# A four-layer hybrid model on one core: the experts' down product with split weights streamed per slot

## The chip, the cores and the metric

The program runs on one core of one Trainium2 chip. The metric is device time in microseconds, the median of the runs shown. The core has five engines with queues of their own: TensorE (PE; its weight loads are listed as PEld), VectorE (DVE), ScalarE (ACT), GpSimd (POOL) and SyncE (SP). They wait for each other through semaphores, and each runs its own instructions strictly in the order in which the program gives them.

## The reference, cut to what matters

The model has 4 x 1024 tokens of width 256 and four layers in a row, each with a residual sum: attention with low-rank adapters, an expert layer, a Mamba-2 layer, and the same expert layer again with the same weights. The expert layer is

```python
x = hidden_states.reshape(-1, d)               # 4096 x 256, normalised
logits = x @ Wr + br                           # 4 experts
probs = softmax(logits)
top_w, top_idx = top_k(probs, 1)               # one expert for each token
g = einsum('td,edf->tef', x, Wg)               # d = 256, f = 1024
u = einsum('td,edf->tef', x, Wu)
h = silu(g) * u
y = einsum('tef,efd->ted', h, Wd)
out = take_along_axis(y, top_idx) * top_w
```

The change concerns the product with `Wd` for the chosen expert, in both expert layers, and where its weights come from.

## The kernel before

`program` runs four phases one after the other: `attention`, `routed_ffn` (names with g1_), `mamba`, `routed_ffn` again (g2_). Each phase writes one instruction list per engine (`@block.sync`, `vector`, `gpsimd`, `scalar`, `tensor`), by hand; no planner is involved in the expert layers. In the profile's rows the names of both expert layers begin with g_.

**The expert layer** starts with a prologue: TensorE turns the tokens, the router's logits are formed, and VectorE works out to which of 35 slots (`SLOTS`) each token belongs. A slot is 128 tokens of one expert; 32 tiles of tokens and up to three partly filled ones give 35. Meanwhile SP loads the gate and up weights (8 MB) and, from L1024, the down weights of all four experts (4 MB) into `w_d`. ScalarE rounds the gate and up weights to the short form F32R (`w_hi`), and VectorE subtracts the rounded part, so that the rest (L1054) stands in F32R in `w_gu`: a full product is then formed from three short ones, high x high, high x low, low x high (`terms`, L1410 on).

Then the 35 slots follow. For slot j:
- POOL `fetch(j)` (L1240) gathers the slot's 128 token rows from DRAM, an indirect DMA with 128 indices.
- VectorE `stats(j)` (L1170 to L1172) forms mean and variance; POOL `root(j)` (through L90) forms the inverse root; VectorE `center(j)` (L1179) normalises.
- TensorE `turn(j)` (L1401) transposes the tokens; VectorE `take(j)` (L1184, L1186) splits them into high and low.
- TensorE `up(j)` (L1419) forms gate and up, 24 products of 512 columns; ScalarE `activate(j)` (L1319) and VectorE `combine(j)` (L1192) form the hidden values.
- TensorE `turn_hidden(j)` (L1441) transposes them in eight pieces into `ps_h`; VectorE copies one half (L1197), ScalarE the other (L1323) to `hid_t`.
- TensorE `down(j)` (L1433): eight products of 256 columns in full F32, each of which TensorE runs as two passes, so 16 instructions per slot. The expert's weights are picked in `w_d` through a register.
- VectorE `result(j)` (L1203) scales and adds the residual; POOL `send(j)` (L1247) scatters the rows to DRAM.

The order on each engine is a software pipeline. TensorE does up(j), down(j-1), turn(j+1), turn_hidden(j). VectorE does

```python
if j + 2 < SLOTS: stats(j + 2)
combine(j)                      # then take(j + 1), hidden(j), result(j - 1)
if j + 2 < SLOTS: center(j + 2)
```

and POOL does root(j+2), send(j-1), fetch(j+3). Four token buffers (`XE`), two result buffers and one buffer of hidden values set how far the engines can run ahead.

**The attention phase** has 16 units of 24 steps (`CORE`). In a step TensorE forms a pair of score products (L854), ScalarE takes two exponentials (L690), POOL masks on the diagonal (L576), and TensorE weighs the values (L870) four steps later; the probabilities stand in a ring of seven. VectorE meanwhile finds maxima of score chunks for later heads (L438, L442). In the last four units no query, key or value work for a later batch is left, so `raw`, `rope`, `x_t`, `xn` and `swapped` are unused after the fifth step of unit 12. POOL's `remainder` (L546) is a subtraction of 128 x 512 values; SP collects sums and results by DMA (`collect`, `gather_sums`, `store_inverse`, `spread_inverse`).

## Time and profile before

| | |
|---|---|
| median of 3 runs | 2194.78 us (2182.81 to 2199.73) |
| the profiled execution | 2185.0 us |
| its span, first to last instruction | 2183.1 us |
| busy: TensorE, VectorE, ScalarE, GpSimd | 1819.3, 1191.3, 822.7, 725.6 us |
| moved by DMA | 161 MB, mean 74 GB/s |
| mean granted TensorE clock | 0.901 of 2.4 GHz |

The busy times of different engines overlap. Idle time of an engine only costs something where the others wait for it. The attention phase ends at about 812 us, the first expert layer runs from 820 to 1245, the Mamba layer to about 1755, the second expert layer to the end.

### The profile page before, as it was taken

How to read it: one execution, taken by the hardware profiler on the slowest of the kernel's cores; microseconds unless marked ns; L12 is line 12 of the kernel's file. 1: busy time of each engine (PE TensorE's matmuls, PEld its weight loads, DVE VectorE, ACT ScalarE, POOL GpSimd, SP SyncE). 2: the span in 40 equal slices, each digit the busy share in tenths (PEclk: the TensorE clock that was granted, in tenths of full speed). 3: DMA queues.
4: the chain of work that ended last, by engine and by line, in shares of the span. 5: the costliest groups of instructions: out<-in, count | busy, mean ns of one | idle time of the engine just before them, and what ended most of it. 6: DMA issues, size and time to landing. Idle time of an engine off the chain costs nothing. (4 is left out here: it accounts for less than half of the span.)

```text
span 2183.1 us, 30159 instructions
## 1 busy us (share of the span) xinstructions
PE 1819.3 (83%) x9520; PEld 1212.1 (56%) x9520; DVE 1191.3 (55%) x2979; ACT 822.7 (38%) x1705; POOL 725.6 (33%) x922
## 2 busy tenths in 40 slices
PE   5368889889888864899999658989898938999997
PEld 3133334434433322788888535747484727888886
DVE  4466676666666508543443356665656685443442
ACT  2036655656665624111111035554646441111111
POOL 2335464464462312222222124333242312222221
PEclk9569989989988855999999969999999978999999
DMA  5522333332442108000000230100101080000000
GB/s 160 174 89 90 119 126 95 122 125 77 134 135 87 39 16 313 22 24 28 26 25 26 70 111 15 43 36 1 78 1 78 1 309 22 26 24 30 25 24 9
DMA packets 90179, 161.23 MB, mean 74 GB/s; under 512 B 23080, under 2 KB 50476, under 8 KB 88880
## 3 DMA queue, kind: packets, MB, share of 16 engines
q1 hardware_dynamic: 71504, 107.39, 14.7%
q0 software_dynamic: 17984, 50.62, 7.2%
q8 instruction: 86, 1.41, 0.3%
q10 hardware_dynamic: 544, 1.31, 0.2%
q14 instruction: 61, 0.50, 0.1%
HBM read 102.52 MB, written 45.48 MB: 68 GB/s over the span
## 5 line engine op out<-in xcount | busy, mean ns | idle before, releaser
L690 ACT ACTIVATE a_probs<-a_ps_e 128x512 f32<-128x512 f32 (+3 forms) x768 | 336.0, 491 | 204.1 <-PE a_ps_e L854 200.9
L438 DVE CUSTOM_DVE_ANT_0 a_ps_m<-a_ps_m,a_causal 128x512 f32<-128x512 f32 (+3 forms) x512 | 239.4, 517 | 97.5 <-PE a_ps_m L841 96.4
L1433 PE MATMUL g_ps_y<-g_w_d,x_res 128*128 x1120 | 253.2, 379 | 2.8 <-DVE x_res L1203 2.8
L854 PE MATMUL a_ps_e<-a_q_st,a_k_st 64*128 64x512 f32 (+3 forms) x768 | 187.9, 480 | 76.4 <-ACT a_probs L690 48.5
L854 PEld LDWEIGHTS a_ps_e<-a_q_st,a_k_st 64*128 64x128 f32 x768 | 79.6, 201 | 289.8 <-ACT a_probs L690 200.5
L1433 PEld LDWEIGHTS g_ps_y<-g_w_d,x_res 128*128 128x128 f32 x1120 | 212.3, 190 | 34.6 <-issue 3.2
L442 DVE TENSOR_REDUCE a_peak<-a_ps_m 128x1 f32<-128x512 f32 x256 | 164.8, 686 | 94.8 <-PE a_ps_m L841 94.1
L841 PE MATMUL a_ps_m<-a_k_st,a_q_st 64*128 64x512 f32 (+3 forms) x768 | 152.7, 399 | 68.8 <-DMA a_k_st<-a_scr_k 28.0
L1323 ACT COPY x_res<-g_ps_h 128x512 f32<-128x512 f32 x70 | 41.1, 587 | 439.2 <-PE g_ps_h L1441 439.2
L576 POOL TENSOR_SCALAR_AFFINE_SELECT a_probs<-a_probs 128x256 f32<-128x256 f32 x256 | 103.9, 408 | 284.1 <-ACT a_probs L690 283.8
L1170 DVE BATCH_NORM_STATS2 g_xe_stats<-x_res 128x6 f32<-128x256 f32 x70 | 29.9, 426 | 295.6 <-DMA x_res<-g_x_rows,g_token_i 295.6
L870 PE MATMUL a_ps_a<-a_probs,a_vals 128*32 128x512 f32 (+3 forms) x1536 | 185.7, 559 | 0.1
L1319 ACT ACTIVATE x_res<-g_ps_g 128x1024 f32<-128x1024 f32 x70 | 71.9, 1028 | 213.8 <-PE g_ps_g L1419 213.8
L841 PEld LDWEIGHTS a_ps_m<-a_k_st,a_q_st 64*128 64x128 f32 x768 | 84.4, 205 | 102.6 <-issue 44.5
L90 POOL TENSOR_TENSOR g_xe_rs<-g_xe_ve,table 128x1 f32<-128x1 f32 x70 | 39.2, 561 | 202.5 <-DVE g_xe_ve L1172 202.5
L1240 POOL DMA_INDIRECT x_res<-g_x_rows,g_token_i x70 | 77.6, 1108 | 84.0 <-DVE g_token_i L1145 63.5
L1192 DVE TENSOR_TENSOR x_res<-x_res,g_ps_u 128x1024 f32<-128x1024 f32 x70 | 85.5, 1221 | 27.3 <-PE g_ps_u L1419 27.3
L1419 PE MATMUL g_ps_g<-g_w_hi,g_xe_hi 128*128 x280 | 95.7, 423 | 1.7 <-DVE g_xe_hi L1184 1.7
L1773 POOL TENSOR_TENSOR m_y<-m_y,m_z_act 128x512 f32<-128x512 f32 x32 | 40.6, 1269 | 157.1 <-DVE m_y L1699 157.1
L1247 POOL DMA_INDIRECT g_y_rows<-x_res,g_token_i x35 | 36.6, 1044 | 168.2 <-DVE x_res L1203 163.4
L1247 POOL DMA_INDIRECT out<-x_res,g_token_i x35 | 36.6, 1044 | 168.1 <-DVE x_res L1203 168.1
L1624 DVE SCALAR_TENSOR_TENSOR m_conv<-m_pre,m_conv_w,m_conv 128x1024 f32<-128x1024 f32 x48 | 70.1, 1460 | 34.9 <-ACT m_conv L1827 34.0
(272 smaller groups left out, 3664.5 us busy)
## 6 DMA issues: line engine op xcount, KB each, us to landing
a_q_st<-a_scr_q POOLq DMA_DIRECT2D x32, 512.0 KB, 4.0
a_k_st<-a_scr_k POOLq DMA_DIRECT2D x32, 512.0 KB, 4.8
m_spread_acs<-m_acs_rows SPq DMA_DIRECT2D x8, 2048.0 KB, 9.7
a_scr_q<-a_high SPq DMA_DIRECT2D x36, 256.0 KB
a_scr_k<-a_high SPq DMA_DIRECT2D x36, 256.0 KB
a_swapped<-a_raw SPq DMA_DIRECT2D x64, 128.0 KB, 2.0
g_w_gu<-L_ffn_Wg SPq DMA_DIRECT2D x8, 1024.0 KB, 9.8
g_w_gu<-L_ffn_Wu SPq DMA_DIRECT2D x8, 1024.0 KB, 12.4
```

The source lines that it names most:

```text
L438: nc.vector.tensor_tensor_reduce(ps_m[:, bank, 0:w], ps_m[:, bank, 0:w], causal[:, 512 - w:], 1.0, MASKED, ALU.add, ALU.max, peak[:, p % 2 ...
L442: nc.vector.tensor_reduce(peak[:, p % 2, r, i, c:c + 1], ps_m[:, bank, 0:w], AX, ALU.max).then_inc(chunk_max, 1)
L576: nc.gpsimd.affine_select(tile, tile, [[0, 2], [1, P]], ALU.is_ge, 0.0, base=0, channel_multiplier=-1).then_inc(masked, 1)
L690: nc.scalar.activation(probs[:, N % RING, r, q0:], ps_e[:, (2 * N + r) % HEAD_BANKS, q0:], ACT.Exp, scale=DH ** -0.5).then_inc(exp_done, 1)
L841: nc.tensor.matmul(banks[r][:, 0:w], q_st[rows(r), p % BUFS, i * P:(i + 1) * P], k_st[rows(r), p % BUFS, 512 * c:512 * c + w], start=True, ...
L854: nc.tensor.matmul(ps_e[:, (2 * N + r) % HEAD_BANKS, q0:], k_st[rows(r), p % BUFS, j * P:(j + 1) * P], q_st[rows(r), p % BUFS, 512 * c + q ...
L870: last = nc.tensor.matmul(ps_a[32 * u:32 * u + 32, q0:], vals[:, b % 2, j, 17 * h:17 * h + 32], probs[:, (U * CORE + 2 * m + u // 2) % RIN ...
L1192: nc.vector.tensor_tensor(hid, gate, ps_u[:].rearrange("p b f -> p (b f)"), ALU.mult).then_inc(hid_ready, 1)
L1240: nc.gpsimd.indirect_dma_start(out=xe[:, j % XE], out_offset=None, in_=x_rows, in_offset=bass.IndirectOffsetOnAxis(ap=token_i[:, j:j + 1], ...
L1247: nc.gpsimd.indirect_dma_start(out=y_rows, out_offset=bass.IndirectOffsetOnAxis(ap=token_i[:, j:j + 1], axis=0), in_=rows[:, j % 2], in_of ...
L1419: last = nc.tensor.matmul(ps[:, c], x[:, d * P:(d + 1) * P], w[:, :, d].rearrange("p a f -> p (a f)"), start=(n == d == 0), stop=(n == len ...
L1433: last = nc.tensor.matmul(ps_y[:, 0:D], hid_t[:, f * P:(f + 1) * P], w_d[:, bass.ds(e, 1), f].rearrange("p a d -> p (a d)"), start=(f == 0 ...
```

## The change

The down product is formed from three short terms like the gate and up products. The split weights don't stay in SBUF: the attention phase prepares them once, in its last four units, in a DRAM table `down_rows` of 512 rows (one for each expert and partition) of 16 KB, in which a row holds, for each of eight tiles, 256 high and 256 low values. For each of four experts, SP loads 1 MB (`load_down`), ScalarE rounds four pieces of 128 x 512 (`round_down`), POOL subtracts four (`lower_down`), and SP stores 2 MB in three DMAs (`store_down`).

In the expert layers the load of `Wd` on SP goes. POOL gathers for each slot the 128 rows of its expert (2 MB, `stream`) by an indirect DMA into one of two buffers; the row numbers come from two new small steps on VectorE. `hidden` is now two copies on ScalarE, which round, and two subtractions on VectorE, each of which waits for its copy. `down` has eight products of 512 columns (high hidden x high and low weights side by side) and eight of 256 (low hidden x high weights); `result` adds both halves in two dependent steps. On VectorE the order becomes center(j+1), combine(j), take(j+1), hidden(j), result(j-1), stats(j+2); on POOL send(j-1), fetch(j+3), stream(j+1), root(j+2).

```diff
 # attention, SP, in the loop over units U and steps n
+                    if U * CORE + n in WD_AT:
+                        load_down(WD_AT[U * CORE + n])
+                    if U * CORE + n - 21 in WD_AT:
+                        store_down(WD_AT[U * CORE + n - 21])
+        WD_AT = {12 * CORE + 10 + 14 * e: e for e in range(EXPERTS)}
+            def load_down(e):
+                sp.wait_ge(low_ready, 4 * 2 * BATCH)
+                if e >= 2:
+                    sp.wait_ge(wd_out, 48 * (e - 1))
+                sp.dma_start(wd_raw[e % 2].rearrange("p (t d) -> p t d", d=D), A["Wd"][e].rearrange("(t p) d -> p t d", p=P)
+                             ).then_inc(wd_in, 16)
+            def store_down(e):
+                sp.wait_ge(wd_less, 4 * (e + 1))
+                sp.dma_start(wd_rows[e, :, :, 1], wd_raw[e % 2].rearrange("p (t d) -> p t d", d=D)).then_inc(wd_out, 16)
+                for k in range(2):
+                    sp.dma_start(wd_rows[e, :, 4 * k:4 * k + 4, 0], wd_high[e % 2][k].rearrange("p (t d) -> p t d", d=D)
+                                 ).then_inc(wd_out, 16)
+            def lower_down(e, k):                      # POOL, steps 11, 13, 15, 17 after the load
+                pool.wait_ge(wd_rounded, 4 * e + k + 1)
+                nc.gpsimd.tensor_tensor(part.bitcast(F32R), part, high_part, ALU.subtract).then_inc(wd_less, 1)
+            def round_down(e, k):                      # ScalarE, steps 8, 10, 12, 14 after the load
+                if k == 0:
+                    act.wait_ge(wd_in, 16 * (e + 1))
+                nc.scalar.copy(high_part.bitcast(F32R), wd_raw[e % 2][:, 512 * k:512 * k + 512]).then_inc(wd_rounded, 1)
...
 # expert layer, SP
-            sp.wait_ge(turned_ps, HALVES)
-            for e in range(EXPERTS):
-                sp.dma_start(w_d[:, e], F["Wd"][e].rearrange("(t p) d -> p t d", p=P)).then_inc(wd_in, 16)
 # VectorE
+            step(nc.vector.tensor_scalar(owner[:, 1, :], owner[:, 0, :], float(P), lanes[:, 0:1], ALU.mult, ALU.add))
+            nc.vector.tensor_copy(row_index[:], owner[:, 1, :]).then_inc(index_ready, 1)
             def hidden(j):
-                dve.wait_ge(ht_ps, j + 1)
-                nc.vector.tensor_copy(hid_t[:, 0:512], ps_h[:, 0]).then_inc(ht_lo, 1)
+                for c in range(2):
+                    dve.wait_ge(ht_hi, 2 * j + c + 1)
+                    some = slice(c * 512, (c + 1) * 512)
+                    nc.vector.tensor_tensor(hid_lo[:, some], ps_h[:, c], hid_hi[:, some].bitcast(F32), ALU.subtract
+                                            ).then_inc(ht_lo, 1)
             def result(j):
-                nc.vector.scalar_tensor_tensor(rows[:, j % 2], ps_y[:, 0:D], scale[:, j:j + 1], xe[:, j % XE], ALU.mult,
-                                               ALU.add).then_inc(row_sb, 1)
+                step(nc.vector.scalar_tensor_tensor(rows[:, j % 2], ps_y[:, 0:D], scale[:, j:j + 1], xe[:, j % XE],
+                                                    ALU.mult, ALU.add))
+                nc.vector.scalar_tensor_tensor(rows[:, j % 2], ps_y[:, D:2 * D], scale[:, j:j + 1], rows[:, j % 2],
+                                               ALU.mult, ALU.add).then_inc(row_sb, 1)
-            center(1)
             weights()
             for j in range(SLOTS):
-                if j + 2 < SLOTS:
-                    stats(j + 2)
+                if j + 1 < SLOTS:
+                    center(j + 1)
                 combine(j)
...
-                    center(j + 2)
+                    stats(j + 2)
 # POOL
+            def stream(j):
+                if j >= 2:
+                    pool.wait_ge(y_ps, j - 1)
+                nc.gpsimd.indirect_dma_start(
+                    out=w_d[:, j % 2].rearrange("p f d -> p (f d)"), out_offset=None, in_=C["wd_rows"],
+                    in_offset=bass.IndirectOffsetOnAxis(ap=row_index[:, j:j + 1], axis=0),
+                    bounds_check=EXPERTS * P - 1, oob_is_err=False).then_inc(streamed[j % 2], 16)
             root(0)
             root(1)
+            for j in range(2):
+                stream(j)
             for j in range(SLOTS):
-                if j + 2 < SLOTS:
-                    root(j + 2)
                 if j >= 1:
                     send(j - 1)
                 if j + 3 < SLOTS:
                     fetch(j + 3)
+                if 2 <= j + 1 < SLOTS:
+                    stream(j + 1)
+                if j + 2 < SLOTS:
+                    root(j + 2)
 # ScalarE
             def hidden(j):
                 act.wait_ge(ht_ps, j + 1)
-                nc.scalar.copy(hid_t[:, 512:1024], ps_h[:, 1]).then_inc(ht_hi, 1)
+                for c in range(2):
+                    nc.scalar.copy(hid_hi[:, c * 512:(c + 1) * 512], ps_h[:, c]).then_inc(ht_hi, 1)
 # TensorE, down(j)
+                w = w_d[:, j % 2]
+                pe.wait_ge(streamed[j % 2], sends(j % 2, j + 1))
                 for f in range(FT):
-                    last = nc.tensor.matmul(ps_y[:, 0:D], hid_t[:, f * P:(f + 1) * P],
-                                            w_d[:, bass.ds(e, 1), f].rearrange("p a d -> p (a d)"), start=(f == 0),
-                                            stop=(f == FT - 1))
+                    if f % 4 == 0:
+                        pe.wait_ge(ht_hi, 2 * j + f // 4 + 1)
+                    nc.tensor.matmul(ps_y[:], hid_hi[:, f * P:(f + 1) * P], w[:, f], start=(f == 0), stop=False,
+                                     skip_group_check=True)
+                for f in range(FT):
+                    if f % 4 == 0:
+                        pe.wait_ge(ht_lo, 2 * j + f // 4 + 1)
+                    last = nc.tensor.matmul(ps_y[:, 0:D], hid_lo[:, f * P:(f + 1) * P], w[:, f, 0:D], start=False,
+                                            stop=(f == FT - 1), skip_group_check=True)
```

## Rows read from the trace of the kernel before

**Rows 1.** Windows: stretch, its us, busy us of each engine, clock, DMA share, GB/s.
```profile
1000.00:1200.00 200.00, 199.37 (x984) 168.93 (x983) 81.11 (x176) 32.31 (x40) 52.13 (x59) 1.00 0.08 26
```

**Rows 2.** One slot in order of time: start, us, engine, line, operation [idle before].
```profile
1010.07 0.38 PE L1401 MATMUL g_ps_x<-table,x_res 128*128 128x128 f32 x2
...
1010.29 1.04 PE L1441 MATMUL g_ps_h<-table,x_res 128*128 128x128 f32 x8
...
1011.09 0.71 PE L1419 MATMUL g_ps_g<-g_w_hi,g_xe_hi 128*128 x2
1011.37 0.59 ACT L1323 COPY x_res<-g_ps_h 128x512 f32<-128x512 f32 x1 [6.31 <-PE g_ps_h L1441]
1011.37 0.69 DVE L1197 COPY x_res<-g_ps_h 128x512 f32<-128x512 f32 x1
...
1011.98 0.47 DVE L1203 SCALAR_TENSOR_TENSOR x_res<-g_ps_y,g_scale,x_res 128x256 f32<-128x256 f32 x1
...
1013.26 1.05 POOL L1247 DMA_INDIRECT g_y_rows<-x_res,g_token_i  x1 [4.47 <-DVE x_res L1203]
...
1014.61 1.02 POOL L1240 DMA_INDIRECT x_res<-g_x_rows,g_token_i  x1 [0.30 <-issue]
...
1016.75 3.62 PE L1433 MATMUL g_ps_y<-g_w_d,x_res 128*128 x16
1017.44 0.43 DVE L1170 BATCH_NORM_STATS2 g_xe_stats<-x_res 128x6 f32<-128x256 f32 x1 [4.67 <-DMA x_res<-g_x_rows,g_token_i]
1017.90 0.18 DVE L1171 BATCH_NORM_AGGREGATE g_xe_mv<-g_xe_stats 128x2 f32<-128x6 f32 x1
...
1018.20 1.22 DVE L1192 TENSOR_TENSOR x_res<-x_res,g_ps_u 128x1024 f32<-128x1024 f32 x1
1018.36 0.56 POOL L90 TENSOR_TENSOR g_xe_rs<-g_xe_ve,table 128x1 f32<-128x1 f32 x1 [2.73 <-DVE g_xe_ve L1172]
...
1020.20 0.38 PE L1401 MATMUL g_ps_x<-table,x_res 128*128 128x128 f32 x2
...
1022.49 0.41 DVE L1179 TENSOR_SCALAR x_res<-x_res,g_xe_mv,g_xe_rs 128x256 f32<-128x256 f32 x1
```

**Rows 3.** TensorE in the Mamba layer, in order of time.
```profile
1503.76 1.90 PE L2020 MATMUL m_ps_y<-m_xdt,m_mix 128*128 128x64 f32 x16
1505.49 0.61 PE L1984 MATMUL m_ps_t<-table,m_xbc 128*128 128x128 f32 x4
```

**Rows 4.** The start of the slots of the first expert layer, in order of time.
```profile
866.98 8.89 DVE L1054 TENSOR_TENSOR g_w_gu<-g_w_gu,g_w_hi 128x2048 fp32r<-128x2048 f32 x4
868.03 2.28 POOL L1240 DMA_INDIRECT x_res<-g_x_rows,g_token_i  x1 [31.82 <-DVE g_token_i L1145]
...
876.70 0.57 POOL L90 TENSOR_TENSOR g_xe_rs<-g_xe_ve,table 128x1 f32<-128x1 f32 x1 [2.16 <-DVE g_xe_ve L1172]
877.31 0.41 DVE L1179 TENSOR_SCALAR x_res<-x_res,g_xe_mv,g_xe_rs 128x256 f32<-128x256 f32 x1 [0.69 <-POOL g_xe_rs L90]
...
878.56 0.42 DVE L1184 CAST g_xe_hi<-g_ps_x 128x256 fp32r<-128x256 f32 x1
...
879.13 1.22 PE L1419 MATMUL g_ps_g<-g_w_hi,g_xe_hi 128*128 x2 [0.60 <-DVE g_xe_hi L1184]
```

**Rows 5.** Attention: POOL and ScalarE in order of time, then a window (columns as in Rows 1).
```profile
644.41 0.56 POOL L558 DMA_DIRECT2D a_k_st<-a_scr_k  x1
644.97 0.42 POOL L576 TENSOR_SCALAR_AFFINE_SELECT a_probs<-a_probs 128x256 f32<-128x256 f32 x1
...
699.57 1.09 ACT L690 ACTIVATE a_probs<-a_ps_e 128x512 f32<-128x512 f32 x2 [0.15 <-PE a_ps_e L854]
...
661.00:763.00 102.00, 85.75 (x571) 36.13 (x569) 64.20 (x205) 63.06 (x149) 33.48 (x70) 0.88 0.20 59
```

**Rows 6.** A window of loads, and DMA issues: KB each, us to landing.
```profile
823.00:828.00 5.00, 4.54 (x23) 4.16 (x21) 4.86 (x29) 2.02 (x2) 2.09 (x2) 0.50 1.00 398
...
x_res<-g_x_rows,g_token_i POOLq DMA_INDIRECT x70, 2.8
```

More of the change, by code:

```diff
@@ L266, in attention, with parts, keep @@
         inverted, normed = sem("inverted"), sem("normed")
+        wd_in, wd_rounded, wd_less, wd_out = (sem(n) for n in ("wd_in", "wd_rounded", "wd_less", "wd_out"))
         def rows(r):
             return slice(64 * r, 64 * r + 64)
+        def parts(blk, i):
+            return high[:, i % 2], low[:, i % 2]
+        def keep(eng, blk, i):
+            eng.wait_ge(low_ready, 4 * blk + i + 1)
+            n, half = i % 2, i // 2
+            to = scr[n][blk % 2, :, :, :, half * 512:(half + 1) * 512]
+            hi, lo = parts(blk, i)
+            for c, part in enumerate(((hi, hi, None, lo), (hi, lo, None, hi))[n]):
+                if part is not None:
+                    eng.dma_start(to[:, c], part).then_inc(scr_out[i % 2], 16)
         block = ctx.enter_context(nc.Block())
@@ L297, in swap @@
                     sp.dma_start(swapped[1 - odd:P:2, i % 2], raw[odd:P:2, i]).then_inc(swap_in[i], 16)
-            def keep(blk, i):
-                sp.wait_ge(low_ready, 4 * blk + i + 1)
-                n, half = i % 2, i // 2
-                to = scr[n][blk % 2, :, :, :, half * 512:(half + 1) * 512]
-                for c, part in enumerate(((high, high, None, low), (high, low, None, high))[n]):
-                    if part is not None:
-                        sp.dma_start(to[:, c], part[:, i % 2]).then_inc(scr_out[i % 2], 16)
             def collect(U, c):
@@ L624, in _ @@
                         remainder((U - 1) // GROUPS * 2 + 2 + (U - 1) % GROUPS // 2, 2 + (1, 4).index(n))
+                    for k in range(4):
+                        if U * CORE + n - 11 - 2 * k in WD_AT:
+                            lower_down(WD_AT[U * CORE + n - 11 - 2 * k], k)
                     if n == 0 and U >= 1 and U + 1 < UNITS:
@@ L722, in _ @@
                             evacuate(e)
+                    for k in range(4):
+                        if U * CORE + n - 8 - 2 * k in WD_AT:
+                            round_down(WD_AT[U * CORE + n - 8 - 2 * k], k)
                     if U >= 1 and n == 2:
@@ L923, in routed_ffn @@
         w_hi = sb("w_hi", [P, EXPERTS, DT, 2 * FF], F32R)
-        w_d = sb("w_d", [P, EXPERTS, FT, D])
+        with nc.sbuf_tensor(name + "later", [P, 4608 + P], F32) as held_later:
+            later = held_later[:]
+        w_d = sb("w_d", [P, 2, FT, 2 * D], F32R)
         w_r = sb("w_r", [P, DT, 32])
@@ L978, in routed_ffn @@
         warm = sb("warm", [P, 1])
-        loaded, saved, cleared, wd_in = (sem(n) for n in ("loaded", "saved", "cleared", "wd_in"))
+        loaded, saved, cleared, index_ready = (sem(n) for n in ("loaded", "saved", "cleared", "index_ready"))
         w_in = [sem(f"w_in{e}") for e in range(EXPERTS)]
@@ L991, in routed_ffn @@
         sent = [C["sems"](f"rows_sent{k}") for k in range(2)]
+        streamed = [C["sems"](f"rows_streamed{k}") for k in range(2)]
         spread, rs_ready, xe_normed, xe_ps, xe_sb, xe_split = (
@@ L1454, in _ @@
                 if j >= 1:
[L1455 removed]
+                    down(j - 1)
                 if j + 1 < SLOTS:
@@ L1458, in _ @@
                 turn_hidden(j)
-            down(SLOTS - 1, expert_of(SLOTS - 1))
+            down(SLOTS - 1)
         ctx.close()
@@ L2112, in program @@
     with ExitStack() as ctx:
+        with ExitStack() as under:
+            hid = [under.enter_context(nc.sbuf_tensor("hidden_" + k, [P, FF], F32R)) for k in ("high", "less")]
         X = ctx.enter_context(nc.sbuf_tensor("x_res", [P, NT, D], F32))
```

37 lines of the change are left out of this document (23 added, 14 removed).

## The prediction

> **What bounds the kernel now.** I read the page first, then the windows by stage, then the time-ordered instructions of one expert slot, then the start and the end of an expert layer. The page shows TensorE as by far the busiest engine, which says little by itself, as stages differ. The windows do say it: in the expert layer from 1000 to 1200 us TensorE is busy 199.37 of 200 us, at a granted clock of 1.00, with DMA at 26 GB/s [rows 1]. So in the expert layers the order of TensorE's work sets the time, and there are 35 slots in each of two layers.
>
> The slot shows it instruction by instruction [rows 2]. From one turn of the tokens (L1401, 1010.07) to the next (1020.20) are 10.13 us without an idle stretch: 0.22 for the turn, 0.80 for the eight transposes of the hidden values (L1441, from 1010.29), 5.66 for the 24 gate and up products (L1419, from 1011.09), 3.45 for the 16 passes of the down product (L1433, from 1016.75). Everything else is off that path. The reader should look at POOL in the same rows: after the result (L1203, ends 1012.45) it sends (1013.26), fetches (ends 1015.63), and then is idle until the variance of the next slot comes; the root (L90) ends 1018.92, and the centring that needs it (L1179, 1022.49) comes 3.6 us later. That slack is what the change spends.
>
> **Part 1: the down product.** It removes 16 passes (3.45 us) and adds 8 products of 512 columns and 8 of 256. The 512-column ones have the form of L1419: 5.66 / 24 = 0.236 us each, 1.89 us. The 256-column ones stand in no row in this number form. The bounds: 0.108 us, which is what a weight load with a short product costs (L2020, 16 in 1505.49 - 1503.76) [rows 3], and 0.216, one of the 16 passes that go, which have 256 columns each (3.45 / 16). I take 0.11, since half of a 512-column product is 0.118 and near the load's cost: 0.88 us. Down is then 2.77 us (bounds 2.75 and 3.62), TensorE's slot 9.45 us (9.43 to 10.30), 0.68 less than now. If nothing else came to bind, that would be 66 x -0.68 = -45 us.
>
> **Part 2: the chain that the new order closes.** VectorE now does per slot: centre(j+1), combine(j), take, hidden(j), result(j-1), statistics(j+2). POOL does send(j-1), fetch(j+3), stream(j+1), root(j+2). So root(j+2) stands behind three indirect DMAs, the first of which waits for result(j-1); centre(j+2) waits for that root and stands ahead of combine(j+1); combine(j+1) is needed by the hidden transposes, whose remainders stand ahead of result(j). That is a loop of one slot. Before, the root was first on POOL and the centring last on VectorE, and it was open. Its length, from the end of one result to the end of the next:
> - result to send 0.81, send 1.05, gap 0.30, fetch 1.02, gap 0.30 [rows 2]: 3.48.
> - The stream: the fetch's 1.03, as it too has 128 indices. The root follows it with no gap, as mask behind DMA does (644.97 right behind 644.41 + 0.56) [rows 5]. Root 0.56, root to centring 0.04 (876.70 + 0.57 to 877.31) [rows 4]: 5.11 so far.
> - Centring 0.41, gap 0.03 (as 1017.44 + 0.43 to 1017.90), combine 1.22 [rows 2], VectorE to TensorE 0.15 (878.56 + 0.42 to 879.13) [rows 4]: 6.92.
> - Transposes to ScalarE 1.08 (1010.29 to 1011.37): 8.00. ScalarE now copies both halves at 0.59 (it did one): first ends 8.59, second 9.21. VectorE's remainder of a half costs what its copy of one did, 0.69: first 8.65 to 9.34, second 9.37 to 10.06. Result in two steps of 0.47 with gaps of 0.03: 11.06 us.
>
> 11.06 is above TensorE's 9.45 and above the present 10.13, so the loop sets the slot, and the down product's gain turns into idle time of TensorE ahead of the turn and of the hidden transposes. 33 such steps per layer: 66 x (11.06 - 10.13) = **+61 us**. The stream's own cost is the unknown. A plain DMA of 128 rows of 4 KB costs POOL 0.56 [rows 5], the lower bound; the other 0.47 of an indirect one would then go by pieces, and a 16 KB row cut into four would cost 0.56 + 4 x 0.47 = 2.44, the upper one. I take 1.03, because the plain DMA moves four times the bytes of the fetch at half its cost, so bytes are not what POOL is paid for. Bounds of the loop 10.59 and 12.47, of the term +30 and +154.
>
> **Part 3: the streamed weights.** 2.1 MB per slot against 26 GB/s now. Loads of this kind run at 398 GB/s [rows 6], 5.3 us, and an indirect fetch of 128 KB lands 2.8 us after issue: 8.1 us. stream(j+1) is issued 3.48 us after result(j-1) and lands 11.6 us after it. Counted from the hidden transposes of slot j, that result ends at 4.14 (the steps above from 6.92 to 11.06) and down(j+1) starts at 11.06 + 0.80 + 5.66 = 17.52, which is 13.4 after the result: it fits in, with 1.8 us to spare. It also closes a longer loop over two slots: 3.48 + 8.1 + down 2.77 + turn 0.22 + 4.14 = 18.7, 9.4 per slot, under 11.06. Only below some 240 GB/s (11.5 us) would it take over. Fetch and send stand on the same queue one slot behind a stream that has landed by then. The Trainium skill (DMA: Bandwidth & Descriptors, Anatomy of one DMA) fits 2.0 us + bytes / 436e3 for such transfers. By it the stream would take 6.8 us and the two-slot loop 8.7 per slot, which speaks more firmly against DMA as the bound than my rows do; no row shows an indirect transfer of that size.
>
> **Part 4: attention.** Added for each of four experts, in its last quarter: a load (1 MB), four ScalarE copies, four POOL subtractions, 2 MB of stores. ScalarE is busy 63 of 102 us there, but where steps are wide it is nearly full: two exponentials take 1.09 with 0.15 of waiting [rows 5]. 16 copies of 0.59 are 9.4 us at most, 0 if the ring of probabilities hides them; I take 6, as the wide steps are most of the time. POOL: 16 x 1.27 = 20 us beside 33 busy of 102, hidden by the four steps that the weighing lags; uncovered, one subtraction holds up a mask by 1.27. Twelve stores and four loads on SP stand ahead of collecting the sums, which is due half a unit (18 us) later: nothing; uncovered, the 6 us of a store, once per expert. The load is issued 8 steps (some 12 us) ahead of its copy and needs 2.6 at the rate above beside a latency like the fetch's 2.8: nothing; if it is late, ScalarE's exponentials queue behind the copy that waits.
>
> **Part 5: start and end of a layer.** Two small steps of VectorE for the indices ahead of the tokens' (0.24 + 0.18 and gaps): 0.5. The 4 MB of Wd per layer is no longer loaded, which frees nothing: the first fetch waits for VectorE (indices at 867, lowering until 875.87), not for data [rows 4]. The first two streams follow the second root and have until the first down, two slots' gate and up products (11.3 us) later, which the first (8.1) makes. At the end of the layer no product hides the chain: one more copy, remainder and result step stand ahead of the last down, 0.59 + 0.69 + 0.50, less the 0.68 of down: +1.1. Together +1.6 a layer, **+3 us**.
>
> **Sum.** 61 + 6 + 3 = +70 us. The profiled execution took 2185.0 us (span 2183.1), so 2255 in its terms; the median of the three runs, 2194.8, is 9.8 above it, which gives 2265.
>
> **The rivals.**
> - *The loop is longer* (the stream dearer, its transfer slower, or POOL held up). Dearer at 2.44: +154, with 9 for the rest, 2358. The first fetch cost 2.28 beside VectorE's lowering, where 1.02 is usual [rows 2, 4], so VectorE can hold POOL's indirect DMAs up; in the loop only the statistics (0.43 + 0.18 + 0.15) fall beside them, at most 0.76 more, 66 x 0.76 = +50, 2315. [...] Chance 0.18.
> - *TensorE remains the bound, and it gets faster.* Place: POOL, between send and root. If an indirect DMA only hands over its work and the root passes at once, the loop loses 3.1 us and is 8.0, TensorE's 9.45 decides: 66 x -0.68 + 9 = -36, 2159. It decides from a loss of 1.61 on; from 0.93 on it is no longer slower in the slots. Against it: mask starts only at the end of the DMA ahead of it [rows 5], and two indirects never overlap [rows 2]. For it: no row shows a computation right behind an indirect one. Chance 0.11.
> - *Half of this*: the loop near the present 10.13, or the down product's remainder terms at the upper bound with a short loop (10.30): 2190 to 2217. Chance 0.09.
> - *The clock.* Longer idle stretches could cost TensorE its clock. The expert layer would have some 1.6 us idle in 11.06; from 661 to 763 us it is busy 86 of 102, a like share, at a mean clock of 0.88, so part of that stretch ran at 1.2 GHz [rows 5]. A slot at 1.2 GHz would be TensorE's again, twice 9.45 or some 19 us long, so each costs 8; it is part of the first rival's 0.18.
>
> **The numbers.** Forecast 0.62, its own range 2235 to 2321 (loop 10.6 to 11.9). About 1% is what a measurement of this kernel can tell from no change. Slower by over 1%: 0.62 + 0.18 = 0.80; within: 0.09; faster: 0.11. The range 2195 to 2350 leaves out the faster case and the dearest streams.
>
> **What would show it.** In the changed profile: sends 11.1 us apart; root right behind the stream, centring 0.04 behind the root, combine right behind that, TensorE idle ahead of L1401 and L1441 with centring and combine as releasers, 1.6 us together; the stream near 1.03 on POOL; down 2.8 us. If sends are 9.5 apart and TensorE has no idle, the loop was wrong; if the down product waits for the stream, the transfer was.

## The result and the profile after

Before took 2192.14 us (median of 4 runs, 2182.81 to 2199.73), after 2250.11 (4 runs, 2245.81 to 2253.36): ratio 1.0261, 95% interval 1.0221 to 1.0300. The change makes the kernel **2.6% slower**. The profiled execution of after took 2245.81 us with a span of 2244.0, against 2185.0 and 2183.1. The forecast was 2265 us, 70 more than before; 58 were measured.

The window of the expert layer that answers to [rows 1], columns as there:

```profile
1000.00:1200.00 200.00, 185.88 (x935) 150.78 (x936) 96.21 (x208) 39.98 (x57) 68.04 (x74) 1.00 0.62 222
```

TensorE was busy 199.37 of these 200 us and is now busy 185.88. It has less to do and waits 14 us, at a full granted clock. DMA went from a share of 0.08 to 0.62 and is still not full. Who makes TensorE wait stands in the groups by line (the instructions and their idle time are those of the whole execution):

```profile
L1501 PE MATMUL g_ps_y<-g_w_d,hidden_high 128*128 128x512 f32 x560 | 145.0, 401 | 8.8 <-DMA g_w_d<-down_rows,g_row_index 8.8
...
L1513 PE MATMUL g_ps_h<-table,x_res 128*128 128x128 f32 x560 | 76.1, 279 | 42.9 <-DVE x_res L1240 42.9
...
L1300 POOL DMA_INDIRECT g_w_d<-down_rows,g_row_index x70 | 70.1, 1001 | 21.2 <-issue 21.2
```

The 70 streamed weights cost 8.8 us of waiting in all. The transposes of the hidden values (L1513) wait 42.9 us for VectorE's gated product (L1240). One slot in order of time, against [rows 2], shows why:

```profile
1025.09 0.48 DVE L1256 SCALAR_TENSOR_TENSOR x_res<-g_ps_y,g_scale,x_res 128x256 f32<-128x256 f32 x1
...
1026.39 1.06 POOL L1307 DMA_INDIRECT g_y_rows<-x_res,g_token_i  x1 [6.39 <-DVE x_res L1256]
...
1027.75 1.02 POOL L1292 DMA_INDIRECT x_res<-g_x_rows,g_token_i  x1 [0.30 <-issue]
1028.15 2.03 PE L1501 MATMUL g_ps_y<-g_w_d,hidden_high 128*128 128x512 f32 x8
1029.08 1.00 POOL L1300 DMA_INDIRECT g_w_d<-down_rows,g_row_index  x1 [0.31 <-issue]
1030.02 1.09 PE L1506 MATMUL g_ps_y<-g_w_d,hidden_less 128*128 128x256 f32 x8
1030.10 0.58 POOL L90 TENSOR_TENSOR g_xe_rs<-g_xe_ve,table 128x1 f32<-128x1 f32 x1
1030.72 0.41 DVE L1227 TENSOR_SCALAR x_res<-x_res,g_xe_mv,g_xe_rs 128x256 f32<-128x256 f32 x1 [4.40 <-POOL g_xe_rs L90]
1031.05 1.21 DVE L1240 TENSOR_TENSOR x_res<-x_res,g_ps_u 128x1024 f32<-128x1024 f32 x1
...
1032.31 1.09 PE L1513 MATMUL g_ps_h<-table,x_res 128*128 128x128 f32 x8 [0.69 <-DVE x_res L1240]
...
1033.44 1.07 ACT L1390 CAST hidden_high<-g_ps_h 128x512 fp32r<-128x512 f32 x2 [6.87 <-PE g_ps_h L1513]
...
1034.06 1.29 DVE L1247 TENSOR_TENSOR hidden_less<-g_ps_h,hidden_high 128x512 fp32r<-128x512 f32 x2 [1.01 <-ACT hidden_high L1390]
...
1035.78 0.48 DVE L1256 SCALAR_TENSOR_TENSOR x_res<-g_ps_y,g_scale,x_res 128x256 f32<-128x256 f32 x1
```

Read it from one L1256 to the next, 10.69 us. In between no step waits for anything but the step before it: send, fetch, stream and root on POOL, centring and gated product on VectorE, transposes, ScalarE's copies, remainders, result. In [rows 2] the centring came 3.6 us after its root; here it starts 0.04 after it (1030.10 + 0.58 to 1030.72), behind a wait of 4.40 us of VectorE.

Where the 60.9 us of the two spans lie, by milestones (before, after): last copy of the attention's sums 792.0, 807.8 (+15.8); first to last send of the first expert layer 339.7, 358.3 (+18.6), of the second 338.9, 358.2 (+19.3); the rest, +7.2, in the starts of the slots (+1.7 and +1.0), the stretch between the layers (+1.7) and the end (+2.7). The 15.8 is not all the change's, as experiments 6 to 12 show.

Of the 34 distances between the sends of a layer only the first 31 have the full length: they take 16.4 us more than before in the first layer and 18.1 in the second. In the last slots no fetch is left, the loop is shorter by the fetch and its gap, and two slots take 9.5 and 9.3 us, less than before (10.1 and 9.9). The very last distance is 7.9 and 7.1 us where it was 4.5: the last down product waits for its stream.

```profile
1270.66 3.78 PE L1501 MATMUL g_ps_y<-g_w_d,hidden_high 128*128 128x512 f32 x8 [4.57 <-DMA g_w_d<-down_rows,g_row_index]
```

It also runs slower than the 2.03 us of the others: the granted clock from 1270.6 to 1275.8 is 0.55.

### The profile page after: what moved, and what is told of

Its sections match the earlier page's. It is cut to its first block and busy times, and to the rows that moved or that the text cites. A ratio compares the mean times of both kernels' runs of the same rounds, so it can differ in the third digit from the quotient of the medians.

```text
span 2244.0 us, 29790 instructions
## 1 busy us (share of the span) xinstructions
PE 1816.0 (81%) x9520; PEld 1177.9 (52%) x9520; DVE 1265.2 (56%) x3123; ACT 864.3 (39%) x1791; POOL 819.6 (37%) x1008
## 3 DMA queue, kind: packets, MB, share of 16 engines
HBM read 245.12 MB, written 53.87 MB: 133 GB/s over the span
## 5 line engine op out<-in xcount | busy, mean ns | idle before, releaser
L900 PE MATMUL a_ps_e<-a_q_st,a_k_st 64*128 64x512 f32 (+3 forms) x768 | 193.2, 494 | 79.6 <-ACT a_probs L727 47.9
L1390 ACT CAST hidden_high<-g_ps_h 128x512 fp32r<-128x512 f32 x140 | 75.3, 590 | 469.6 <-PE g_ps_h L1513 469.6
L887 PE MATMUL a_ps_m<-a_k_st,a_q_st 64*128 64x512 f32 (+3 forms) x768 | 157.5, 413 | 66.3 <-DMA a_k_st<-a_scr_k 25.9
L916 PE MATMUL a_ps_a<-a_probs,a_vals 128*32 128x512 f32 (+3 forms) x1536 | 192.0, 577 | 0.1
L1227 DVE TENSOR_SCALAR x_res<-x_res,g_xe_mv,g_xe_rs 128x256 f32<-128x256 f32 x70 | 28.9, 413 | 283.6 <-POOL g_xe_rs L90 283.6
L1501 PE MATMUL g_ps_y<-g_w_d,hidden_high 128*128 128x512 f32 x560 | 145.0, 401 | 8.8 <-DMA g_w_d<-down_rows,g_row_index 8.8
L1247 DVE TENSOR_TENSOR hidden_less<-g_ps_h,hidden_high 128x512 fp32r<-128x512 f32 x140 | 90.2, 686 | 71.5 <-ACT hidden_high L1390 71.3
L1501 PEld LDWEIGHTS g_ps_y<-g_w_d,hidden_high 128*128 128x128 f32 x560 | 106.4, 191 | 35.3 <-DMA g_w_d<-down_rows,g_row_index 9.5
L1513 PE MATMUL g_ps_h<-table,x_res 128*128 128x128 f32 x560 | 76.1, 279 | 42.9 <-DVE x_res L1240 42.9
L1240 DVE TENSOR_TENSOR x_res<-x_res,g_ps_u 128x1024 f32<-128x1024 f32 x70 | 85.0, 1214 | 14.1 <-PE g_ps_u L1486 14.1
```

What stands on the lines that cost most here:

```text
L887: nc.tensor.matmul(banks[r][:, 0:w], q_st[rows(r), p % BUFS, i * P:(i + 1) * P], k_st[rows(r), p % BUFS, 512 * c:512 * c + w], start=True, ...
L900: nc.tensor.matmul(ps_e[:, (2 * N + r) % HEAD_BANKS, q0:], k_st[rows(r), p % BUFS, j * P:(j + 1) * P], q_st[rows(r), p % BUFS, 512 * c + q ...
L916: last = nc.tensor.matmul(ps_a[32 * u:32 * u + 32, q0:], vals[:, b % 2, j, 17 * h:17 * h + 32], probs[:, (U * CORE + 2 * m + u // 2) % RIN ...
L1240: nc.vector.tensor_tensor(hid, gate, ps_u[:].rearrange("p b f -> p (b f)"), ALU.mult).then_inc(hid_ready, 1)
L1247: nc.vector.tensor_tensor(hid_lo[:, some], ps_h[:, c], hid_hi[:, some].bitcast(F32), ALU.subtract).then_inc(ht_lo, 1)
L1501: nc.tensor.matmul(ps_y[:], hid_hi[:, f * P:(f + 1) * P], w[:, f], start=(f == 0), stop=False, skip_group_check=True)
```

## The experiments

Ratios are to runs of the kernel before on the same chip as the experiment; the median of before was 2196.35, 2195.07 and 2195.8 us in the three groups (1 to 4, 5 to 8, 9 to 12). "A slot" is the distance of two sends.

**1. Root first** on GpSimd, the rest of the change kept.

```
             for j in range(SLOTS):
+                if j + 2 < SLOTS:
+                    root(j + 2)
                 ...send(j - 1), fetch(j + 3), stream(j + 1)
-                if j + 2 < SLOTS:
-                    root(j + 2)
```

> The changed kernel with one difference: on GpSimd the root of slot j+2 comes ahead of the send, the fetch and the stream, in place of behind them. Theory (the one-slot loop result, send, fetch, stream, root, centring, combine sets the slot): the loop opens, the root ends about 1.4 us after a result in place of 5.1. But the stream now follows the statistics, the root, the send and the fetch: issued 4.3 us after the result, it lands 8.5 us later, and the two-slot loop result, stream, down product, result is 19.7 us, 9.86 per slot, in place of 10.69 in the changed kernel. 66 x -0.83 = -55 us: about 2195, ratio 1.00 to the kernel before, sends 9.9 us apart, with TensorE waiting about 0.4 us per slot for the stream. Rival A (the added work of VectorE and ScalarE sets the slot, whatever GpSimd's order): 10.7 per slot, 2250. Rival B (the stream's transfer sets the slot): 10.7 or more, since the stream is issued no earlier than before; 2250 or above.

Measured: 2224.71 us (2214.38 to 2230.78), ratio 1.0116 (1.0081 to 1.0151). The first-to-last sends give 10.17 us a slot (922.84 to 1268.47 over 34, the short last ones among them); the same measure gives 10.54 in after and 9.99 in before. So the order on GpSimd carries a good half of the loss, but what is left is more than expected. POOL and TensorE in this kernel:

```profile
1004.30 1.18 POOL L1307 DMA_INDIRECT g_y_rows<-x_res,g_token_i  x1 [0.20 <-issue]
...
1007.12 1.01 POOL L1300 DMA_INDIRECT g_w_d<-down_rows,g_row_index  x1 [0.31 <-issue]
...
1013.80 1.17 POOL L1307 DMA_INDIRECT g_y_rows<-x_res,g_token_i  x1 [0.20 <-issue]
...
1015.55 2.13 PE L1501 MATMUL g_ps_y<-g_w_d,hidden_high 128*128 128x512 f32 x8 [0.60 <-DMA g_w_d<-down_rows,g_row_index]
```

The down product at 1015.55 waits for the stream issued at 1007.12, 8.43 us earlier. Sends are mostly 9.5 us apart, then 10.4 to 13.2 (1033.66, 1045.23, 1054.72, 1067.90): the loop of the stream over two slots is next in line. The prediction had put it at 9.4 a slot, with the stream issued 3.48 us behind a result; here it is 4.41 (1002.71 to 1007.12), as statistics and root stand between, and a short pair of slots is 19.9 (1004.30 to 1024.16). In the long ones the transfer is slower and the clock falls: the stream of 1048.06 is waited for until 1057.73, 9.67 us later, the granted clock is 0.80 in the 2.3 us behind that wait, and the distance of the sends is 13.2.

**2. Stream first**: order stream, root, send, fetch. The stream waits only for the down product that frees its buffer, not for the result behind it.

```
             for j in range(SLOTS):
+                if 2 <= j + 1 < SLOTS:
+                    stream(j + 1)
+                if j + 2 < SLOTS:
+                    root(j + 2)
                 ...send(j - 1), fetch(j + 3)
```

> The changed kernel with one difference: the order on GpSimd is stream(j+1), root(j+2), send(j-1), fetch(j+3). Theory: both loops are open; the stream is issued about 0.6 us after the hidden transposes start and lands 6 us before the down product that needs it; TensorE is without idle again, at 9.47 to 9.5 us per slot (0.22 + 0.80 + 5.66 + 2.80). 66 x -1.2 = -80 us, and the 4.3 us wait for the stream at the end of each layer goes, with the slow clock behind it: about 2160, ratio 0.985 to the kernel before. Rival A (VectorE and ScalarE): 10.7 per slot, 2250. Rival B (DMA traffic of 2.1 MB a slot holds TensorE or the fetches up): between 9.9 and 10.7.

Measured: 2170.31 us (2168.93 to 2172.70), ratio 0.9882 (0.9864 to 0.9900), **faster than both kernels**, 1.2% under before. The window, and three of its rows:

```profile
1000.00:1200.00 200.00, 200.00 (x1055) 169.53 (x1054) 112.44 (x233) 44.41 (x64) 79.02 (x84) 1.00 0.70 249
```

```profile
1035.22 1.00 POOL L1300 DMA_INDIRECT g_w_d<-down_rows,g_row_index  x1 [2.22 <-PE g_ps_y L1506]
...
1044.71 1.00 POOL L1300 DMA_INDIRECT g_w_d<-down_rows,g_row_index  x1 [2.19 <-PE g_ps_y L1506]
...
1050.47 2.03 PE L1501 MATMUL g_ps_y<-g_w_d,hidden_high 128*128 128x512 f32 x8
```

TensorE never rests, the slot is 9.49 us (44.71 less 35.22), and the stream of 1035.22 is used 15.25 us later, where it lands after 8.8 (median of 70). In the slots the shorter down product is worth what the prediction said it could be (9.45); in after the loop had eaten it. Of the whole time it gives 26 us.

**3. Small rows**: the stream moves 2 KB per row instead of 16 KB from the third slot on. This leaves the down product with old weights.

```
-                    out=w_d[:, j % 2]..., in_=C["wd_rows"],
+                    out=w_d[:, j % 2]...[:, 0:512], in_=C["wd_rows"].rearrange("r (s c) -> (r s) c", c=512),
```

> The changed kernel, but from slot 2 on each stream moves rows of 2 KB in place of 16 KB (an eighth of the bytes, same number of indices and same instruction count); the down product then runs with weights that are mostly those of the first two slots, so the numbers are others. Theory: the transfer is not on the one-slot loop, GpSimd pays per index: stream 1.0 us on GpSimd, 10.69 us per slot as in the changed kernel, total within 10 us of it (2240 to 2250; some us less from the end of each layer, where the last down product waits 4.3 us for its stream). Rival B (the transfer or the traffic sets the slot): down to 9.5 to 9.9 per slot, 2170 to 2195. Rival C (GpSimd pays by bytes): the stream falls to about 0.6 and the slot to 10.3, 2224.

Measured: 2240.76 us (2236.65 to 2243.03), ratio 1.0208 (1.0190 to 1.0226). The slot is 10.69 (sends at 1033.92 and 1044.61), POOL's share of the stream is unchanged at 1.00, the landing fell from 8.5 to 3.4 us:

```profile
1036.61 1.00 POOL L1301 DMA_INDIRECT g_w_d<-down_rows,g_row_index  x1 [0.31 <-issue]
1037.63 0.59 POOL L90 TENSOR_TENSOR g_xe_rs<-g_xe_ve,table 128x1 f32<-128x1 f32 x1
```

An eighth of the traffic moves neither POOL nor the slot. The bytes are not what makes the slot longer. The whole is still 9 us less than after: 5 of them are the last slots of the two layers (the first to last send takes 355.9 and 355.3 us), where the down product no longer waits for its stream.

**4. No low products**: the eight 256-column products of the remainders are left out of the down product, and what they add is missing from the result.

```
-                for f in range(FT):
-                    ...
-                    last = nc.tensor.matmul(ps_y[:, 0:D], hid_lo[...], w[:, f, 0:D], ...)
```

> The changed kernel without the eight products of the low part of the hidden values with the high weights (that term is left out of the result); everything else, the copies and subtractions too, stays. TensorE does 0.93 us less per slot. Theory: TensorE is not the bound, the slot stays 10.69 and the idle time of TensorE grows by 0.93: total within 5 us of the changed kernel (2245 to 2252), unless the longer idle stretches cost TensorE its clock. Rival D (TensorE's products still set the slot): 66 x -0.93 = -61 us, 2189.

Measured: 2251.71 us (2245.49 to 2259.71), ratio 1.0267 (1.0239 to 1.0295). Slot 10.70 (1014.64, 1025.34, 1036.04), TensorE busy 171.62 of 200. 0.93 us a slot taken from TensorE gives nothing back.

**5. One result step**: the loop is shortened by one of its own steps.

```
-                step(nc.vector.scalar_tensor_tensor(rows[:, j % 2], ps_y[:, 0:D], ..., xe[:, j % XE], ...))
-                nc.vector.scalar_tensor_tensor(rows[:, j % 2], ps_y[:, D:2 * D], ..., rows[:, j % 2], ...)
+                nc.vector.scalar_tensor_tensor(rows[:, j % 2], ps_y[:, 0:D], ..., xe[:, j % XE], ...)
```

> The kernel after, with the two result steps of VectorE made into one: scale times the high-weight half of PSUM plus the input row. What the low halves of the weights give is left out of the result (TensorE still computes it). Theory A (the loop from result to send to the next result sets the slot, 10.69 us in the profile after): the step taken out of the loop has its start 0.51 us before the other's, so the slot falls to 10.18 us, 67 slots by 0.51 = 34 us less, about 2216 us, ratio to before 1.011. TensorE, with 9.49 us of work in a slot, is still not the bound. Rival B (something else keeps 10.69 us a slot, the stream's landing for one): slot unchanged, 2250 us, ratio 1.026. Rival C (the stream's issue comes 0.5 us earlier after the down product's end, but a landing of 8.4 to 9.7 us already binds, as in the kernel with the root first): a slot of about 10.3 to 10.7 us that alternates, 2225 to 2250 us.

Measured: 2216.72 us (2213.17 to 2225.77), ratio 1.0121 (1.0075 to 1.0167). Sends:

```profile
1019.40 1.06 POOL L1305 DMA_INDIRECT g_y_rows<-x_res,g_token_i  x1 [5.88 <-DVE x_res L1254]
...
1029.59 1.06 POOL L1305 DMA_INDIRECT g_y_rows<-x_res,g_token_i  x1 [5.88 <-DVE x_res L1254]
...
1039.77 1.06 POOL L1305 DMA_INDIRECT g_y_rows<-x_res,g_token_i  x1 [5.87 <-DVE x_res L1254]
```

10.19 and 10.18 us. Half a microsecond off a small engine's step is half a microsecond off each slot, while 0.93 off TensorE (experiment 4) was nothing: that is how a loop shows itself.

**9. Both old orders**, statistics first on VectorE and root first on GpSimd, with the streamed three-term product kept.

```
             for j in range(SLOTS):
-                if j + 1 < SLOTS:
-                    center(j + 1)
+                if j + 2 < SLOTS:
+                    stats(j + 2)
                 ...
                     result(j - 1)
                 if j + 2 < SLOTS:
-                    stats(j + 2)
+                    center(j + 2)
 # GpSimd
             for j in range(SLOTS):
+                if j + 2 < SLOTS:
+                    root(j + 2)
                 ...send(j - 1), fetch(j + 3), stream(j + 1)
-                if j + 2 < SLOTS:
-                    root(j + 2)
```

> The kernel after with both orders of before put back: on VectorE the statistics two slots ahead first and the centring last, on GpSimd the root first and then send, fetch and stream. What is left of the change is the streamed split weights, the down product in three terms and the table. Theory A (the new GpSimd order carries the serial loop; with the root first only the loop of the stream over two slots is left, as in the kernel with the root first, 10.17 us a slot, whichever order VectorE has): a slot of 10.1 to 10.3 us, about 2225 us, ratio 1.010 to 1.016. Rival B (the statistics moved last on VectorE are what made the slot longer): a slot of 10.0 us or less and below 2210 us. Rival C (statistics first hold up VectorE while the product waits): 10.7 us or more and above 2245 us.

Measured: 2269.74 us (2267.54 to 2284.28), ratio 1.0348 (1.0296 to 1.0400). My theory A was wrong here and rival C right: slots of 11.0 us (1027.37, 1038.34, 1049.27, 1060.32). VectorE:

```profile
1015.08 0.48 DVE L1256 SCALAR_TENSOR_TENSOR x_res<-g_ps_y,g_scale,x_res 128x256 f32<-128x256 f32 x1
...
1017.73 1.02 POOL L1293 DMA_INDIRECT x_res<-g_x_rows,g_token_i  x1 [0.30 <-issue]
...
1020.57 0.43 DVE L1218 BATCH_NORM_STATS2 g_xe_stats<-x_res 128x6 f32<-128x256 f32 x1 [4.69 <-DMA x_res<-g_x_rows,g_token_i]
...
1021.33 1.22 DVE L1240 TENSOR_TENSOR x_res<-x_res,g_ps_u 128x1024 f32<-128x1024 f32 x1
```

The statistics at the head of a slot wait for a fetch that was issued after the last result (1015.56 + 5.0 to the landing), and the gated product stands behind them. The same wait is in [rows 2] (4.67 ahead of L1170), where it was harmless: result, fetch, statistics, gated product, one copy and one result step close within TensorE's 10.13. With one more copy, remainder and result step they do not; this is a reading of the rows, and no run takes one of these steps out of this order. Against experiment 1 (ratio 1.0116) the statistics moved last are worth 2.3%, some 50 us.

**10. The old order on VectorE alone**, GpSimd's as in after (the diff is that of 9 without GpSimd's part).

> The kernel after with VectorE's order of before alone: statistics first, centring last; GpSimd's order stays send, fetch, stream, root. Theory A (loop from result over send, fetch, stream, root, centring to the gated product; the statistics, 0.83 us on VectorE, now stand between the centring and the gated product and so inside the loop, where in the kernel after they lie in GpSimd's shadow): the slot becomes 10.69 + 0.77 = about 11.45 us, 67 by 0.77 = 51 us more than after, about 2300 us, ratio 1.049. Rival B (the statistics are done before GpSimd's root comes free, so nothing changes): 10.7 us, 2250 us, ratio 1.026. Rival C (statistics first wait for a fetch that has not landed): over 11.6 us.

Measured: 2300.13 us (2294.47 to 2307.63), ratio 1.0477 (1.0435 to 1.0520); sends at 1032.62, 1044.08 and 1055.54, 11.46 apart. Both figures are those of theory A: what is put into the loop is paid once per slot.

Experiments 9, 1, 10 and after are the four combinations of old and new orders, all with the new product: ratio 1.0348 with both old orders, 1.0116 with VectorE's new one alone, 1.0477 with GpSimd's alone, 1.0261 with both. GpSimd's new order costs 1.3 to 1.5%, VectorE's gains 2.2 to 2.3%, and both together are 0.9% better than both old ones. The new product has more steps outside TensorE, and none of these four orders closes its loops within the 10.13 us of before; that of experiment 2 does.

**6, 7 and 8. The attention's part alone**, in the kernel before: the whole preparation of the table, its computing half, its transfer half.

```
+            def load_down(e): ...           # 6, 8
+            def store_down(e): ...          # 6, 8
+            def round_down(e, k): ...       # 6, 7
+            def lower_down(e, k): ...       # 6, 7
```

> The kernel before with one part of the change alone: in the attention the table of split down weights is prepared (8 loads, 32 rounding copies of ScalarE, 32 subtractions of GpSimd, 24 stores), but nothing reads it; the expert layers are those of before. Nothing of the result is left out. The profile after had the last copy of the attention 15.8 us later than before; 4.4 us of that were there before the first operation of the table, 11.4 came behind it. Theory A (the table's work costs the attention 11 us, and the loop of the expert layers all the rest): last copy at about 803 to 808 us, time +11 us, ratio 1.005. Rival B (the attention's time only scatters with TensorE's granted clock, the work is free as it lies beside TensorE's): last copy at 792 to 797 us, ratio 1.000 to 1.002. Rival C (it costs the 15.8 us in full or more): ratio 1.007 or above.

> As the kernel with the table's preparation alone, but without its 8 loads and 24 stores: the 32 copies of ScalarE and 32 subtractions of GpSimd run at the same places, on whatever lies in the buffers; nothing reads what they make. Theory A1 (ScalarE is the engine that paces these units, and its 32 copies are what costs): the same as the kernel with the whole preparation within 3 us. Theory A2 (the traffic costs: 16.8 MB in and 33.6 MB out beside the attention's own, or SyncE's queue held by the waits): no more than 3 us over the kernel before, ratio 1.000 to 1.001. If A1 and A2 each hold a part: between.

> The other half: the 8 loads and 24 stores of the table's preparation in the kernel before, without the rounding copies and the subtractions; what is stored is not the split weights, and nothing reads it. Theory A1 (ScalarE's copies cost): as the kernel before within 3 us, ratio 1.000 to 1.001. Theory A2 (the traffic costs): as the kernel with the whole preparation within 3 us. The two halves together should give what the whole gives, if the parts do not hide each other.

The counts in these three texts are twice too high: the table needs 4 loads, 16 copies, 16 subtractions and 12 stores, and what is written to DRAM in the whole execution rises from 45.48 to 53.87 MB, by 8.4 MB and not 33.6. In 8 the stores wait for the next load, since there are no subtractions to wait for.

Measured: the whole 2207.80 us (2198.58 to 2217.48), ratio 1.0055 (1.0022 to 1.0089); the computing half 2204.87 (2195.46 to 2216.23), 1.0036 (1.0005 to 1.0067); the transfer half 2201.74 (2193.93 to 2215.13), 1.0054 (1.0025 to 1.0084). The whole costs 12 us (5 to 20). By the intervals the transfer half costs 5 to 18, the computing half 1 to 15; by medians 7 and 10, which is more than the whole, but within the intervals. Neither half seems to be free, and which of them weighs more stays open. How far such small differences carry is seen in experiment 12: the same file once more came out 4.7 us below its reference.

**11. The same with nothing left of the table's work, and 12. the kernel before again.** 11 keeps the buffers and semaphores, 12 is the unchanged file.

> The kernel with the table's preparation alone, with all of its operations and transfers taken out: what is left is the kernel before with a few unused buffers and semaphores. Theory A (the table's work costs about 12 us, by traffic at least): ratio 1.000, interval around 1, within 4 us of the kernel before. Rival B (what the kernels with the table, with its computing half and with its transfer half have in common, code and places, costs the 7 to 12 us that each of them showed): ratio 1.003 to 1.006. The profile gives a second look at where the last copy of the attention lies without any table: 792.0 us in the profile before, 804.9 to 814.5 us in all with some of the table's work, of which up to 11 us were there before the table's first operation.

> The kernel before itself, unchanged, for a second profile of it: its profiled execution took 2185.0 us, 10 us under its median over 19 runs. Theory A (the profiled execution was one of the fast ones, and its attention ended early as TensorE's granted clock fell otherwise): ratio 1.000 within 0.003, the last copy of the attention between 793 and 803 us here, and the slots as in the first profile (9.99 us each). Rival B (792 us is what before gives each time): 791 to 793 us again, and the 13 to 22 us of the kernels with a table are the table's cost.

Measured: 11 took 2194.17 us (2186.97 to 2209.74), ratio 0.9995 (0.9970 to 1.0020); 12 took 2191.13 (2186.55 to 2205.11), ratio 0.9976 (0.9944 to 1.0008). So the edits around the work cost nothing. But the profiles of these two, from 700 to 750 us, first 11 and then 12:

```profile
700.00:750.00 50.00, 43.52 (x259) 16.33 (x259) 35.71 (x113) 29.21 (x71) 15.85 (x34) 0.71 0.26 79
```

```profile
700.00:750.00 50.00, 40.53 (x308) 16.32 (x300) 40.76 (x134) 36.11 (x82) 17.00 (x35) 1.00 0.22 65
```

With the same work to do, one execution was granted 1.00 in this stretch and the other 0.71, and got through 308 against 259 of the recorded matmuls. The last copy of the attention came at 795.5 us in 12, at 810.0 in 11, which has no table (the profiled execution of 11, 2209.74 us, is the slowest of its ten). In after it came at 807.8 with a clock of 0.79 in that stretch. One profile of each kernel can't tell what the attention's part costs: with the same work its end lies 14 us apart. The medians can, within their intervals, and they say 12.

## Why the prediction came out as it did

- **The down product** (part 1): predicted 2.77 us. Measured 1028.15 to 1030.02 for the wide ones, 1.87, and 0.93 for eight narrow ones without a wait (913.51 to 914.44), 2.80. TensorE's slot, predicted 9.45, is 9.49 in experiment 2, where it binds. Taking 0.11 for a narrow product rather than the upper bound of 0.216 was right (0.116).
- **The loop** (part 2): right in every link; the sum was 0.37 too long (11.06 against 10.69). From the result's end to the centring's start 5.11 was predicted and 5.15 measured (1025.57 to 1030.72). What was mis-sized is the handing on behind it, where I had added single durations and gaps. The gated product starts 0.33 after the centring and not 0.44 (0.08 before the centring's listed end, 1030.72 + 0.41 to 1031.05), the transposes 1.26 after the gated product and not 1.37, and the first result step 1.21 after the first remainder and not 1.44: the second remainder is not held up, two of them take 1.29 together, and ScalarE's two copies 1.07, not 1.21. TensorE's idle time, 1.6 in the prediction, is 10.69 - 9.49 = 1.20 a slot.
- **The number of slots** (part 2): taken as 33 a layer by 0.93, 61 us. Measured are 31 full distances and two short ones: 16.4 + 18.1 less 2.5, 32 us. The two short ones I had not seen: without a fetch the loop falls below TensorE's work. That 33 by 0.56, 18.5, looks like the 18.6 of the first layer is chance; the 18.6 has the end of the layer in it.
- **The stream's price on POOL**: taken 1.03, measured 1.00, and experiment 3 shows the reason given, that POOL isn't paid by bytes.
- **The streamed transfer** (part 3): predicted to land after 8.1 us with 1.8 to spare; it lands after 8.5 (median of 70) and is used after 9.84 (1029.08 to the next down product at 1038.92), so 1.3 to spare as a rule. Not bound, as predicted, but it was near: in the first layer two streams of the loop, that of 1029.08 among them, landed only after 9.6 and 9.7. "9.4 per slot" for the loop over two slots was near for an undisturbed transfer (a short pair in experiment 1 gives 9.93, of which 0.47 a slot is its later issue), but not for what the slower transfers make of it, 10.17 over the layer. By the fit in the Trainium skill (DMA: Bandwidth & Descriptors, Anatomy of one DMA) this transfer was estimated at 6.8 us; the measured 8.5 decides, and that fit erred further to the short side than my rows did. One case was missed: the last slot of a layer has no neighbour to hide the stream, and its down product waits 4.57 us for it in the first layer and 4.26 in the second, which is the whole 8.8 of the groups above. With the slower clock behind these waits the ends of the layers cost 3.4 and 2.6 us, where part 5 had 1.1 each.
- **The attention** (part 4): predicted +6 with 9.4 at most, measured +12 (5 to 20) by medians. The step that looks wrong is "Twelve stores and four loads on SP ... nothing": the interval of experiment 8, the transfers alone, begins at 5 us. That is hardly more than the same file differed by in experiment 12, so it is likely and not shown; I had asked who queues behind the transfers, and by what road they cost is open.
- **Starts and ends** (part 5): predicted +3. By milestones, in single profiles, the ends of the layers cost +6.0 and the rest +7.2, together 13.
- **The sum**: 32 + 12 + 13 = 57 against 58 measured between the medians. Predicted 61 + 6 + 3 = 70. That it came within 12 us is in part luck: the slots were put 29 too high, attention and ends 6 and 10 too low.
- **The rivals**: a dearer stream was refuted (1.00); the clock did not fall in the slots (1.00), only behind the waits at the ends of the layers (0.55). TensorE as the bound came true only in experiment 2, where the stream and the root no longer wait for the result; its price was then 2170, where I had 2159 for it.

## What to carry to other kernels

When an operation is moved in one engine's queue, write down the closed path through all engines from that operation to its own next turn: here a root of 0.58 us, moved behind a send that waits for a result, closed a loop of 10.69 us round an engine that needed 9.49. Do it for the old order too when the work in it changes: with the new product, the old orders gave 11.0. The cure here is not a faster step but an order in which each instruction stands ahead of those that wait for something later than it does: stream (free after the down product), root (after the statistics), send and fetch (after the result). And a difference of one profile against one profile in a stretch where TensorE's granted clock wanders is no measurement; take it from medians, with a kernel that has the work taken out beside it, and with the same file run twice to see how far medians differ.

## What the runs showed of the hardware

- An indirect DMA of 128 rows occupies POOL for 1.00 us whether a row has 2 KB or 16 KB; three of them in a row are 0.30 us apart, and a computation right behind one starts within 0.02 (1029.08 + 1.00 to 1030.10).
- From issue to landing such a DMA took 2.8 us (median) with rows of 1 KB, 3.4 with 2 KB and 8.5 with 16 KB (8.3 at the least; 13.4 for the second of the two at the start of a layer, issued 1.4 us behind the first).
- A send that runs beside VectorE's centring takes 1.18 us (1004.30 in experiment 1) where 1.06 is usual. The Trainium skill (SBUF — State Buffer, the box on the "DVE blocks DMA" trap) has VectorE keep POOL from writing descriptors while it runs an operation in a two-port mode; the trace agrees in direction, at 0.12 us a send, but no run shows that the centring is such an operation.
- The first three fetches of a layer, beside VectorE's subtractions of 128x2048 (L1054, a TENSOR_TENSOR), took 2.28, 1.75 and 1.88 us in before where 1.02 is usual. No run takes the subtractions away, so that they are the cause is likely and not shown.
- In the kernel of experiment 9, when TensorE had stood idle for 1.99 us, the eight transposes took 1.59 us where 1.09 is usual in this kernel, and the next pair of products 1.20 where it is 0.71:

```profile
1011.12 1.59 PE L1514 MATMUL g_ps_h<-table,x_res 128*128 128x128 f32 x8 [1.99 <-DVE x_res L1240]
...
1012.36 1.20 PE L1487 MATMUL g_ps_g<-g_w_hi,g_xe_hi 128*128 x2
```

  The granted clock was 1.00 up to that idle stretch, 0.51 from 1012.36 to 1015.03, near the lower of its two levels, 1.2 GHz, and 1.00 again from 1015.0 on. In after, with 0.69 us of idle time ahead of each slot's transposes, it stayed at 1.00.
